# x added inside TensorE's projections instead of on VectorE: the recurrent layer's first stage

## The reference, cut to what matters

```python
xprev = jnp.pad(x, ((0, 0), (1, 0), (0, 0)))[:, :T]
xx = xprev - x
xxx = x + xx * time_maa_x
mix = jnp.tanh(xxx @ time_maa_w1.T).reshape(B, T, 4, -1)
deltas = jnp.einsum('btfd,fcd->fbtc', mix, time_maa_w2)
xrg, xwa, xk, xv = x[None] + xx[None] * (time_maa + deltas)
r = xrg @ receptance.T
g = jnp.tanh(xrg @ gate_w1.T) @ gate_w2.T
k = xk @ key_w.T
kk1 = jnp.tanh(xk @ time_kkk_w1.T)
mk1 = xk @ mk_w1.T
v = xv @ value.T
w1 = jnp.tanh(xwa @ time_decay_w1.T)
a1 = xwa @ time_aaa_w1.T
ma1 = xwa @ ma_w1.T
```

## Time and profile before

| | |
|---|---|
| median of three runs | 3026.3 us (3023.74 to 3031.96) |
| the profiled execution's own time | 3024.9 us |
| its span, first to last instruction | 3023.2 us |
| mean granted TensorE clock | 0.891 |
| busy: TensorE, VectorE, ScalarE, GpSimd | 80%, 72%, 56%, 33% of the span |
| the changed stage | about 45 to 321 us of the span |

### The profile page before, as it was taken

How to read it: one execution, slowest core, us unless ns; L and a number is a source line. 1 busy time by engine, 2 the same in 40 slices (tenths; PEclk the granted TensorE clock), 3 DMA queues, 4 the chain that set the end, 5 groups by cost and what they waited for, 6 DMA issues and landing times. The chain is left out here.

```text
span 3023.2 us, 37535 instructions
## 1 busy us (share of the span) xinstructions
PE 2430.5 (80%) x10280; PEld 1063.9 (35%) x10280; DVE 2177.2 (72%) x5978; ACT 1700.5 (56%) x3085; POOL 1012.6 (33%) x979
## 2 busy tenths in 40 slices
PE   6665478885769999769999989968778888868887
PEld 2211266662334444333333333323331111224443
DVE  6999499993675665555555646668659999567776
ACT  4455244533646666441211248845569999777775
POOL 0222589971244544140000024400020000038886
PEclk8777567767879999889999989989889999989999
DMA  3112676415366665331111123300031111011110
GB/s 127 56 56 70 156 131 112 87 25 139 120 169 125 114 128 110 110 110 32 27 32 32 27 44 93 84 4 0 0 110 42 44 44 44 21 34 35 39 39 25
DMA packets 295846, 211.39 MB, mean 70 GB/s; under 512 B 155320, under 2 KB 263784, under 8 KB 295144
## 3 DMA queue, kind: packets, MB, share of 16 engines
q1 hardware_dynamic: 257696, 191.80, 24.3%
q0 software_dynamic: 19712, 14.96, 3.8%
q10 hardware_dynamic: 18256, 2.52, 0.5%
HBM read 136.18 MB, written 62.52 MB: 66 GB/s over the span
## 5 line engine op out<-in xcount | busy, mean ns | idle before, releaser
L3103 ACT ACTIVATE ca_pw<-ca_ps,ca_mx 128x512 f32<-128x512 f32 x512 | 342.5, 930 | 9.0 <-DVE ca_mx L3139 9.0
L2977 DVE CUSTOM_DVE_ANT_0 mx_sums<-mx_ps,w_w2f 128x512 f32<-128x512 f32 (+3 forms) x512 | 220.4, 486 | 155.8 <-PE mx_ps L2955 155.8
L3139 DVE TENSOR_REDUCE ca_mx<-ca_ps 128x1 f32<-128x512 f32 x512 | 311.6, 680 | 1.2 <-PE ca_ps L3069 1.2
L2934 PE MATMUL gm_ps<-gm_h,w_w2f 128*128 128x512 f32 x512 | 245.4, 612 | 0.0
L3103 ACT ACTIVATION_READ_ACCUMULATOR ca_pw<-ca_ps,ca_mx 128x1 f32 x512 | 230.8, 451 | 0.0
L3069 PE MATMUL ca_ps<-qs,ks 128*128 128x512 bf16 x512 | 175.7, 395 | 49.7 <-ACT ca_pw L3103 33.1
L2665 ACT ACTIVATE ta_pw<-ta_ps,w_cst 128x1280 f32<-128x1280 f32 x128 | 168.0, 1321 | 35.3 <-PE ta_ps L2546 35.1
L3009 ACT ACTIVATE gm_h<-gm_ps,w_w2f 128x512 f32<-128x512 f32 x64 | 44.0, 688 | 253.2 <-PE gm_ps L2934 253.2
L2384 ACT ACTIVATE at_pw<-at_ps 128x1280 f32<-128x1280 f32 x128 | 154.8, 1236 | 29.4 <-PE at_ps L2349 29.3
L2804 DVE TENSOR_TENSOR ta_pw<-ta_pw,w_cst 128x384 f32<-128x384 f32 x128 | 70.7, 553 | 134.7 <-ACT ta_pw L2665 132.9
L2711 POOL DMA_INDIRECT Acc<-XN,f_idx x64 | 104.4, 1631 | 157.3 <-DVE XN L2775 142.6
(11 more groups left out here) (575 smaller groups left out, 6291.9 us busy)
## 6 DMA issues: line engine op xcount, KB each, us to landing
Pd<-s_p SPq DMA_DIRECT2D x48, 384.0 KB, 3.1
ex_w<-e_w SPq DMA_DIRECT2D x48, 256.0 KB
Qd<-rp_q SPq DMA_DIRECT2D x4, 2048.0 KB, 9.6
ss_ellb<-Rd SPq DMA_DIRECT2D x32, 256.0 KB, 3.3
ta_qs<-Pd SPq DMA_DIRECT2D x32, 192.0 KB
ta_ks<-Pd SPq DMA_DIRECT2D x32, 192.0 KB
Pd<-cs_p SPq DMA_DIRECT2D x16, 384.0 KB, 2.5
GX<-Qd SPq DMA_DIRECT2D x44, 128.0 KB
```

The source lines that it names most:

```text
L2934: last = pe.matmul(mps[:, f, :], W(("h1", "h2")[n - 2])[:, j * 512 + f * 128:j * 512 + (f + 1) * 128], src[:, j, :], start=(j == 0), stop= ...
L2977: last = v.tensor_tensor_reduce(out=sums[:, u, at:at + n], in0=ps[:, u, at:at + n], in1=K["w2f"]("down")[:, T - n:T], scale=-1.0, scalar=3 ...
L3103: act.activation(pw[:, h % BUF, jk, :], ps[:, (h * NB + jk) % BANKS, :], ACT.Exp, bias=mx[:, h % H, jk:jk + 1], accum_out=z[:, h % H, jk:j ...
L3139: v.tensor_reduce(mx[:, h % H, jk:jk + 1], ps[:, q % BANKS, :], AX.X, ALU.max, negate=True).then_inc(S["top"], 1)
```

## The change

The mixture is not formed any more. L206 writes the mixed difference alone, straight into `xf`; the four additions of x (L212) with their wait are gone. Since each projection is linear, TensorE adds the projection of x itself: the new helper `mixed` issues the product of the weights with x (read from `XN` through `halves`) and behind it the product of the same weights with the mixed difference, into the same bank. Seven matmuls for each lane become pairs. The semaphore `f1` counts one step for each iteration instead of two.

```diff
@@ VectorE
                 for a in range(LANES):
-                    x = halves(i, a)
                     v.wait_ge(S["delta"][a], i + 1)
                     if i:
                         v.wait_ge(S["pairs"][a], i - 1)
                     for f in range(4):
-                        last = v.scalar_tensor_tensor(out=t[:, a, f, :], in0=ps[:, a, f, :],
+                        last = v.scalar_tensor_tensor(out=xf[:, a, f, :], in0=ps[:, a, f, :],
                                                       scalar=W("maa")[:, f:f + 1], in1=xp[:, a, :],
                                                       op0=ALU.add, op1=ALU.mult)
-                    last.then_inc(S["f1"][a], 1)
-                    v.wait_ge(S["f1"][a], 2 * i + 1)
-                    for f in range(4):
-                        last = v.tensor_tensor(split(xf[:, a, f, :]), split(t[:, a, f, :]), x, ALU.add)
                     last.then_inc(S["xf"][a], 1)
...
-                    v.wait_ge(S["f1"][a], 2 * i + 2)
+                    v.wait_ge(S["f1"][a], i + 1)
@@ TensorE
+            def mixed(out, w, i, a, f, stop=True):
+
+                pe.matmul(out, W(w), halves(i, a), start=True, stop=False)
+                return pe.matmul(out, W(w), xf[:, a, f, :], start=False, stop=stop)
+
...
                     pe.wait_ge(S["xf"][a], i + 1)
-                    pe.matmul(ps[:, a, 0, :], W("receptance"), xf[:, a, 0, :], start=True, stop=True)
-                    pe.matmul(ps[:, a, 1, :], W("gate_w1"), xf[:, a, 0, :], start=True, stop=True)
-                    pe.matmul(ps[0:64, a, 2, :], W("kkk_mk_w1"), xf[:, a, 2, :], start=True, stop=True)
-                    pe.matmul(ps[:, a, 3, :], W("decay_aaa_ma_w1"), xf[:, a, 1, :],
-                              start=True, stop=True).then_inc(S["lowps"][a], 1)
+                    mixed(ps[:, a, 0, :], "receptance", i, a, 0)
+                    mixed(ps[:, a, 1, :], "gate_w1", i, a, 0)
+                    mixed(ps[0:64, a, 2, :], "kkk_mk_w1", i, a, 2)
+                    mixed(ps[:, a, 3, :], "decay_aaa_ma_w1", i, a, 1).then_inc(S["lowps"][a], 1)
...
-                    pe.matmul(ps[:, a, 1, :], W("key_w"), xf[:, a, 2, :], start=True, stop=True)
-                    pe.matmul(ps[:, a, 2, :], W("key_w"), xf[:, a, 2, :], start=True, stop=False)
+                    mixed(ps[:, a, 1, :], "key_w", i, a, 2)
+                    mixed(ps[:, a, 2, :], "key_w", i, a, 2, False)
...
-                    pe.matmul(ps[:, a, 0, :], W("value"), xf[:, a, 3, :],
-                              start=True, stop=True).then_inc(S["vps"][a], 1)
+                    mixed(ps[:, a, 0, :], "value", i, a, 3).then_inc(S["vps"][a], 1)
```

## The result

The changed kernel is slower: 3056.49 us median of four runs (3055.11 to 3066.17) against 3025.52 (3023.74 to 3031.96), ratio 1.0097 (95% interval 1.0084 to 1.011). A second set of runs gave 3057.48 and 1.0104 (1.009 to 1.0119). The forecast was 3054, range 3044 to 3066. The first profiled execution is the longest of its kernel (3066.2, span 3064.4); the stage itself took the same in it as in a second profiled one with a span of 3053.8 (304.4 and 304.3 us), so the stage is read from it and its total is not.

What follows compares the result with a forecast made beforehand. The path through TensorE's projections and ScalarE's chain was taken as the bound: per iteration +10.3 - 2.5 = +7.8 us, 4 x 7.8 = 31.2, less 2.0 for the clock, +29.2. Forecast 3054 us, range 3044 to 3066.

Steps and rivals of the forecast that it cites:

- What bounds the stage: Recurrent layer's first stage: path runs L206/L212, TensorE's projections, ScalarE L379 to L398, then L231; expert choice lies beside it.
- The added products: TensorE's projections: twelve added matmuls on the path per iteration, 0.86 us each, 10.3 us; the seventh per lane costs nothing.
- I take no surcharge: TensorE reading x from XN in 8-byte steps was to cost nothing over a contiguous read.
- The half-rate rival: TensorE reads strided x at half rate: another 4 x 10.3 = 41 us, 3095; 8 in 100.
- The earlier start: Lane 0's L212 leaves the path, so TensorE starts the projections 2.5 us earlier in each iteration.
- The clock: TensorE's granted clock at the projections: half chance it stays up in iterations 1 to 3, some loss in 0; -2.0 us.
- the flat 1.75: Time in us given back in each of iterations 1 to 3 if the clock stays up at the projections.
- a sign against me: A granted clock of 0.50 for more than 4 us of the projections would show the forecast wrong.
- the 1.2 that I had called the most: Iteration 0: work starting 2.5 us earlier inside the low-clock stretch may lose up to 1.2 us more.
- What was late next: VectorE stands some 11 us at L220 waiting for ScalarE's sigmoids; the +7.8 us shift per iteration passes on in full.
- VectorE as the bound: Rival: VectorE bounds the stage, so its 5.0 us per iteration come back whole, -20 us, 3005; 4 in 100.
- A cheaper second product: Rival: second matmul on the same weights costs 0.43 us, +11 less 2, 3034; 5 in 100.

Runs made afterwards that it cites:

- the extra passes: Three more MAX8 passes over the expert choice's table on VectorE per iteration, added to the changed kernel (1.0101 to before) and to the kernel before (1.0063).
- the VectorE half: Against the changed kernel, each projection stays one matmul, without the product with x; L212 is still gone. Ratio to before 0.9957, stage -10.1 us.
- with x contiguous: Changed kernel, but the products with x read 512 contiguous values of XN, so x is added to the wrong tokens. Ratio to before 1.0102.
- the TensorE half: TensorE as changed, VectorE as before with L212 kept, so x is counted twice. Ratio to before 1.0152, stage +44.8 us.

## Why the prediction was right

*What bounds the stage.* Right. The path through TensorE and ScalarE sets it, with VectorE close beside: shown by the two halves (VectorE's work gone, half of it returned; TensorE's work added, all of it paid) and by the extra passes (free after, 4.9 of 6.9 us paid before).

*The added products.* Twelve pitches on the path; the mechanism is right, the size was 0.5 us too small. At full clock the stretch grows from 17.4 us (iteration 2 of the VectorE half, which has before's matmuls) to 28.2, 10.8 per iteration instead of 10.3: the 0.86 us held for the partner, and the 8-byte step costs 0.04 in each product with x. "I take no surcharge" was the term off, by 2 us in all. The half-rate rival fell. Two products into one bank cost nothing more: with x contiguous the products of a pair follow each other at 0.86 us, as L334 and L335 did in before. By the Trainium skill ("SBUF — State Buffer", section "Door 1: The DMA port swizzle") the step should also have been free, as two values share a 16-byte line. The measurement of 612 against 592 ns decides against that for TensorE.

*The earlier start.* 2.5 us predicted, 2.54 measured (offset 5.32 to 2.78).

*The clock.* -2.0 predicted, -2.7 measured, from half-clock time in the stretches of 9.0 us instead of 14.3. Of the three iterations at half a chance, one lost and two kept the clock; the two gave back 1.7 and 2.3 us (before had 4.6 us at half clock in iteration 3, which the flat 1.75 didn't hold), 4.0 against the 2.6 forecast. Iteration 0 held 5.6 us at half clock, more than the 4 us that I had named as a sign against me, and lost 1.3 us more than before (2.8 instead of 1.5): just over the 1.2 that I had called the most, and twice the 0.6 in the sum. That the total came near is in part luck, since the two misses partly cancel.

*The sum.* 4 x 10.8 - 4 x 2.54 - 2.7 = +30.3, against +30.5 in the stage and +29.2 forecast. The surcharge (+1.9) and the clock's larger gift (-0.7) partly cancel. TensorE's stretches were to be 27 to 29 us; they were 28.2 where the clock stayed up, and 30.8 and 29.8 where it fell. The same account gives the other runs: for the TensorE half 43.2 + 1.6 = 44.8, for the VectorE half -10.2 + 0.1 = -10.1.

*What was late next.* The wait at the sigmoids is 11.7 us in iteration 1 and 11.4 on average where 11 was said; the iterations after are 77.1, 76.1 and 74.4 us where 75 was said, which follows the stretches. Their sum grows by what the stretches grow less the earlier start, so nothing was absorbed behind them.

*The rivals.* VectorE as the bound would have shown in the VectorE half alone as -20 us; it gave -10. A cheaper second product would have shown as a pitch under 0.86; none was. Both fell.

## What to carry to other kernels

An engine at 95% busy is not yet the bound: look whether it waits at all, and for whom, and follow that chain. Moving work from it is paid on the other engine at that engine's pitch: here 0.61 us of VectorE was exchanged for 0.86 to 0.90 of TensorE for each user, and a mixture with two or three users costs that many. What was worth having was the earlier start, and it could be had without the products, by releasing each mixture by itself; a product with x paid only where TensorE stood waiting or nobody waited for its result, and its gain was seen in the stage only once VectorE was the bound.

Differences of 2 us in such a kernel can be lost in where the clock falls. Read the stage and the clock in the trace, not only the total.

## What the runs showed of the hardware

- TensorE's granted clock can fall after an idle time of only 1.6 us, while it already works again: in the changed kernel it works for 2.4 us, idles for 1.6, starts at 136.22 and has half the clock from 136.40 us on. It stayed up behind the same work and idle time in the next two iterations. What it costs is readable at once: a stretch of 28.17 us at full clock took 29.83 with 3.4 us at half.
- An fp32 matmul record whose moving operand steps by 8 bytes takes 612 ns instead of 592. VectorE's L212 showed no such price: 686 ns, against 692 for L223 on contiguous tiles.
- VectorE's addition of two operands in SBUF (L211, 128x512 fp32) took 1.27 us while GpSimd's additions (L297, L299) ran, and 0.69 us without them, in each of the three kernels that release the mixtures one by one.
